# A graph layer on one core: late weights held back, p rows four tiles ahead of q rows, logits split on ScalarE, three double chunks in the tail

## The reference

```python
h = relu(layernorm(x))                                   # x: 256 x 1024
feat = concat([h[src], h[dst]], axis=1)                  # 8448 edges
e_hh = relu(feat[:128] @ W_hh + b_hh)                    # 2048 x 1024 each
e_oo = relu(feat[128:768] @ W_oo + b_oo)
e_ho = relu(feat[768:] @ W_ho + b_ho)
logit = concat([e_hh, e_oo, e_ho]) @ W_a + b_a
alpha = softmax of logit over the edges with one dst
z = segment_sum(alpha * h[src], dst)
h_new = relu(concat([h, z])[:64] @ W_hn + b_hn)
o_new = relu(concat([h, z])[64:] @ W_on + b_on)
x = x + concat([h_new, o_new])
h2 = relu(layernorm(x))
W = zeros(1024, 1024).at[src, dst].add(edge_weight)      # ids are below 256
out = x + h2 @ W.T + bias
```

## Time and profile before

| | us |
|---|---|
| median of 3 runs | 349.29 |
| lowest, highest | 348.75, 351.31 |
| the profiled execution's own time | 351.62 |
| its span, first to last instruction | 349.1 |

### The profile page before, as it was taken

How to read it: one execution, slowest core, us unless ns; L and a number is a source line. 1 busy time by engine, 2 the same in 40 slices (tenths; PEclk the granted TensorE clock), 3 DMA queues, 4 the chain that set the end, 5 groups by cost and what they waited for, 6 DMA issues and landing times.

```text
span 349.1 us, 4052 instructions
## 1 busy us (share of the span) xinstructions
PE 312.1 (89%) x1335; PEld 196.7 (56%) x1335; DVE 262.4 (75%) x475; ACT 161.5 (46%) x343; POOL 161.7 (46%) x148
## 2 busy tenths in 40 slices
PE   0899999998999999999999999999899677479993
PEld 0687688653566665666666665566345535343331
DVE  4737448558927999998899989888975799693315
ACT  3773441642353555485445755535253545424101
POOL 3200077066423787777777777888863300000000
PEclk9999999999999999999999999999999896569997
DMA  7997789999999999999999999999999999970003
GB/s 271 347 353 247 257 324 412 395 279 416 409 408 410 410 408 410 408 410 415 410 409 410 409 414 411 409 408 410 410 409 407 408 410 410 407 318 3 0 0 121
DMA packets 34089, 122.05 MB, mean 350 GB/s; under 512 B 3978, under 2 KB 4362, under 8 KB 34068
## 3 DMA queue, kind: packets, MB, share of 16 engines
q0 software_dynamic: 19008, 69.21, 50.1%
q1 hardware_dynamic: 13668, 47.33, 35.5%
q10 hardware_dynamic: 1392, 5.24, 3.7%
HBM read 115.49 MB, written 6.29 MB: 349 GB/s over the span
## 4 chain that ended last, share of the span: by engine, by line
PE 48%; DMA 23%; POOL 15%; issue 6%; DVE 4%; ACT 2%; POOLq 0%; ACTq 0%; DVEq 0%; SPq 0%
DMA Gp<-p_ho,ids 16%; PE psG L740 12%; PE psG L878 12%; POOL Gq L308 8%; POOL Gp L296 7%; DMA W<-weights 5%; PE psG L846 5%; PE psG L946 4%; PE psW L790 4%; PE psA L790 3%; PE psB L790 2%; PE psG L891 1%; PE psG L896 1%; PE psG L933 1%; DMA xs<-x 1%
## 5 line engine op out<-in xcount | busy, mean ns | idle before, releaser
L308 POOL DMA_INDIRECT Gq<-q_ho,ids x60 | 75.8, 1263 | 54.5 <-DVE Gp L570 28.3
L570 DVE TENSOR_TENSOR Gp<-Gp,Gq 128x1024 f32<-128x1024 f32 x65 | 79.3, 1220 | 21.5 <-DMA Gp<-p_ho,ids 12.7
L296 POOL DMA_INDIRECT Gp<-p_ho,ids x60 | 66.3, 1105 | 44.9 <-DMA p_ho<-T 26.9
L878 PE MATMUL psG<-W,hT 128*128 128x512 f32 x192 | 84.6, 592 | 0.0
L574 DVE SCALAR_TENSOR_TENSOR Gp<-Gp,wa 128x1024 f32<-128x1024 f32 x65 | 79.0, 1215 | 0.1
L410 ACT ACTIVATE RL<-ohs,lgh 128x256 fp32r<-128x256 f32 x66 | 32.9, 499 | 63.9 <-DVE lgl L617 50.7
L878 PEld LDWEIGHTS psG<-W,hT 128*128 128x128 f32 x192 | 35.4, 190 | 40.1 <-issue 40.1
L398 ACT ACTIVATE RW<-ohs,ewh 128x256 fp32r<-128x256 f32 x66 | 33.1, 502 | 45.2 <-DVE ohs L561 29.1
L790 PE MATMUL psA<-RL,ohd 128*128 128x256 f32 x240 | 37.2, 307 | 12.8 <-ACT RL L410 12.6
L790 PE MATMUL psW<-RW,ohd 128*128 128x256 f32 x264 | 46.0, 298 | 0.1
L790 PEld LDWEIGHTS psA<-RL,ohd 128*128 128x128 f32 x240 | 33.3, 206 | 16.2 <-ACT RL L410 14.4
(11 more groups left out here) (147 smaller groups left out, 334.8 us busy)
## 6 DMA issues: line engine op xcount, KB each, us to landing
W<-weights SPq DMA_DIRECT2D x72, 512.0 KB
Gp<-weights SPq DMA_DIRECT2D x8, 512.0 KB, 15.0
xs<-x SPq DMA_DIRECT2D x2, 512.0 KB, 3.7
h_rows<-h ACTq DMA_DIRECT2D x1, 1024.0 KB, 4.7
p_ho<-T ACTq DMA_DIRECT2D x2, 512.0 KB, 4.5
q_ho<-T ACTq DMA_DIRECT2D x2, 512.0 KB, 6.4
p_oo<-T ACTq DMA_DIRECT2D x1, 1024.0 KB
q_oo<-T ACTq DMA_DIRECT2D x1, 1024.0 KB
```

What stands on the lines that cost most here:

```text
L296: nc.gpsimd.indirect_dma_start(out=Gp[:, i % NP, :], out_offset=None, in_=p_oo if t <= OO_TILES else p_ho, in_offset=bass.IndirectOffsetOn ...
L308: nc.gpsimd.indirect_dma_start(out=Gq[:, i % NQ, :], out_offset=None, in_=q_oo if t <= OO_TILES else q_ho, in_offset=bass.IndirectOffsetOn ...
L570: nc.vector.tensor_tensor(Gp[:, i % NP, :], Gp[:, i % NP, :], Gq[:, i % NQ, :], ALU.add).then_inc(s_sum, 1)
L878: last = nc.tensor.matmul(psG[:, 2 * t + half, :], hT[:, k, t * P:(t + 1) * P], W[:, s, half * HALF:(half + 1) * HALF], start=u != 1 and k ...
```

## The change

- `PACE` places 29 jobs instead of 30: one double chunk ahead of each of lots 16, 17 and 18, none ahead of lots 19 and 20, one ahead of each of 21 and 22, and three in the tail.
- SP waits for 56 adds (`LATE_TILES`) ahead of the loads of double chunk 3 (`LATE_TOP`), and for 61 adds (`HN_TILES`) ahead of `hn_w`. SP's order of loads is the same.
- POOL issues twelve p gathers, eight q gathers, and then `q_rows(i)` and `p_rows(i + 4)` in turn.
- `lot_split` leaves DVE. ScalarE copies the lot's logits to a rounded high part, uses the unrounded ones as the scale of the first product (its output is rounded), and makes each low part as an activation of its own. DVE's wait for the products of two lots before now stands ahead of the lot's adds.
- b_a is added to the `off` tables (one more DVE operation in `few_counts`, an activation in place of a multiply in `guard_counts`) instead of to the logits.

```diff
--- before.py
+++ after.py
@@ -51,7 +51,7 @@
 PLAIN = 3 * KC
 JOBS = 4 * KC
 CHUNKS = SPLIT + HH + PLAIN + 2 * KC
-PACE = [2, 2, 2, 2] + [2, 2, 1, 2, 1] + [2, 2, 2, 2] + [2, 1, 1, 1, 1]
+PACE = [2, 2, 2, 2] + [2, 2, 1, 2, 1] + [2, 2, 2, 2] + [1, 1, 1, 0, 0, 1, 1]
 JOBS_IN = [0] * (HH_LOT + 1) + PACE + [0] * (NLOTS - HH_LOT - 1 - len(PACE))
 
 FREED = len(GATHERED) - NP
@@ -66,6 +66,8 @@
 
 
 FREED_Q = len(GATHERED) - NQ
+
+LATE_TOP, LATE_TILES, HN_TILES = 3, 56, 61
 assert FREED_Q % NQ + 3 <= NQ
 assert ROW_SLOT + NT <= NP
 
...
@@ -233,9 +235,12 @@
                     sp.wait_ge(s_lo, q - WSLOTS + 1)
                 else:
                     sp.wait_ge(s_wused, uses_before(q))
+                if q == SPLIT + HH + PLAIN + 2 * LATE_TOP:
+                    sp.wait_ge(s_sum, LATE_TILES)
                 load(q)
                 if q == 2 * WSLOTS:
                     sp.dma_start(wa[:, :], w_a.broadcast_to((P, D))).then_inc(s_wa, 16)
+            sp.wait_ge(s_sum, HN_TILES)
             for k in range(KC):
                 sp.wait_ge(s_used, FREED + k + 1)
                 sp.dma_start(hn_w[k], weights[(CHUNKS + k) * P:(CHUNKS + k + 1) * P, :]).then_inc(s_hn, 16)
@@ -311,11 +316,12 @@
 
             for i in range(NP):
                 p_rows(i)
-            for i in range(NP):
+            for i in range(NQ):
                 q_rows(i)
-            for i in range(NP, len(GATHERED)):
+            for i in range(NQ, len(GATHERED)):
                 q_rows(i)
-                p_rows(i)
+                if i - NQ + NP < len(GATHERED):
+                    p_rows(i - NQ + NP)
 
         @block.scalar
         def _(act):
@@ -399,18 +405,31 @@
                                                     ACT.Copy, scale=val[:, t:t + 1].bitcast(f32))
                     last.then_inc(s_wprod, 1)
 
+            def logit_product(g, i, half, val):
+                n = LTH[LOTS[g][i]]
+                if half == 0 and n >= LRING:
+                    act.wait_ge(s_placed, n - LRING + 1)
+                return nc.scalar.activation(RL[:, n % LRING, half, :], ohs[:, (ENTRY[g] + i) % RING, :].bitcast(f32),
+                                            ACT.Copy, scale=val[:, g % 2, i:i + 1])
+
             def logit_products(g):
 
-                act.wait_ge(s_split, g + 1)
-                for i, t in enumerate(LOTS[g]):
-                    n = LTH[t]
-                    if n >= LRING:
-                        act.wait_ge(s_placed, n - LRING + 1)
-                    for half, val in enumerate((lgh, lgl)):
-                        last = nc.scalar.activation(RL[:, n % LRING, half, :],
-                                                    ohs[:, (ENTRY[g] + i) % RING, :].bitcast(f32), ACT.Copy,
-                                                    scale=val[:, g % 2, i:i + 1].bitcast(f32))
-                    last.then_inc(s_lprod, 1)
+                size, first = len(LOTS[g]), LTH[LOTS[g][0]]
+                if LOTS[g][0]:
+                    act.wait_ge(s_used, PLACE[LOTS[g][-1]] + 1)
+                else:
+                    act.wait_ge(s_hh, 1)
+                nc.scalar.copy(lgh[:, g % 2, 0:size], lg[:, g % 2, 0:size]).then_inc(s_lgh, 1)
+                logit_product(g, 0, 0, lg)
+                act.wait_ge(s_lgh, g + 1)
+                for i in range(size):
+                    nc.scalar.activation(lgl[:, g % 2, i:i + 1], lgh[:, g % 2, i:i + 1].bitcast(f32), ACT.Identity,
+                                         bias=lg[:, g % 2, i:i + 1], scale=-1.0).then_inc(s_lgl, 1)
+                for i in range(size):
+                    if i:
+                        logit_product(g, i, 0, lg)
+                    act.wait_ge(s_lgl, first + i + 1)
+                    logit_product(g, i, 1, lgl).then_inc(s_lprod, 1)
 
             def guard_counts():
 
@@ -419,7 +438,7 @@
                 nc.scalar.activation(inv[:, :, :], psC, ACT.Relu, bias=minus[:, 0:1]).then_inc(s_cm, 1)
                 nc.scalar.activation(off[:, :, :], psC, ACT.Relu, bias=unit[:, 0:1], scale=-1.0).then_inc(s_cm, 1)
                 act.wait_ge(s_cm, 2)
-                nc.scalar.mul(off[:, :, :], off[:, :, :], NEG).then_inc(s_cm, 1)
+                nc.scalar.activation(off[:, :, :], off[:, :, :], ACT.Identity, bias=bar[:, 0:1], scale=NEG).then_inc(s_cm, 1)
 
             def lot_weights(g):
                 if LOTS[g][0] > OO_TILES:
@@ -591,6 +610,8 @@
 
             def lot_logits(g):
 
+                if g >= 2:
+                    dve.wait_ge(s_lprod, LTH[LOTS[g - 2][-1]] + 1)
                 for k, t in enumerate(LOTS[g]):
                     if t and k:
                         total(PLACE[t])
@@ -604,26 +625,13 @@
                     else:
                         hh_logit(col)
 
-            def lot_split(g):
-
-                size = len(LOTS[g])
-                if LOTS[g][0]:
-                    dve.wait_ge(s_used, PLACE[LOTS[g][-1]] + 1)
-                else:
-                    dve.wait_ge(s_hh, 1)
-                if g >= 2:
-                    dve.wait_ge(s_lprod, LTH[LOTS[g - 2][-1]] + 1)
-                chain(nc.vector.tensor_scalar(lgh[:, g % 2, 0:size], lg[:, g % 2, 0:size], bar[:, 0:1], None, ALU.add))
-                nc.vector.scalar_tensor_tensor(out=lgl[:, g % 2, 0:size], in0=lg[:, g % 2, 0:size], scalar=bar[:, 0:1],
-                                               in1=lgh[:, g % 2, 0:size].bitcast(f32), op0=ALU.add, op1=ALU.subtract
-                                               ).then_inc(s_split, 1)
-
             def few_counts():
 
                 dve.wait_ge(s_few, 2)
                 chain(nc.vector.tensor_scalar(inv_few[:, :, :, :], few[:, :, :, :], 1.0, None, ALU.max))
                 chain(nc.vector.reciprocal(inv_few[:, :, :, :], inv_few[:, :, :, :]))
                 chain(nc.vector.tensor_scalar(off_few[:, :, :, :], few[:, :, :, :], 0.5, NEG, ALU.is_lt, ALU.mult))
+                chain(nc.vector.tensor_scalar(off_few[:, :, :, :], off_few[:, :, :, :], bar[:, 0:1], None, ALU.add))
 
             def few_max():
 
@@ -649,7 +657,6 @@
             for g in range(NLOTS):
                 lot_logits(g)
                 lot_start(g + 1)
-                lot_split(g)
                 if g - LAST_OO == 1:
                     few_max()
                 elif g - LAST_OO == 2:
```

More of the change, by code:

```diff
@@ L151, in gnn_block @@
         lgh = sb("lgh", [P, 2, LOT], f32r)
-        lgl = sb("lgl", [P, 2, LOT], f32r)
+        lgl = sb("lgl", [P, 2, LOT], f32)
         brow, ew = shared(("brow", [LOW0 + 32, D], f32), ("ew", [P, ET], f32))
@@ L193, in gnn_block @@
         s_ewh, s_bh, s_bl = sem("weights_high"), sem("biases_high"), sem("biases_low")
-        s_hh, s_split = sem("hh_logit"), sem("logits_split")
+        s_hh, s_lgh, s_lgl = sem("hh_logit"), sem("logits_high"), sem("logits_low")
         s_ohs, s_ohd = sem("src_onehot"), sem("dst_onehot")
```

## The result

| | before | after |
|---|---|---|
| median, us | 350.22 (4 runs, 348.75 to 351.31) | 356.50 (4 runs, 355.03 to 358.50) |
| span of the profiled execution | 349.1 | 353.3 |
| its own time | 351.62 | 355.07 |

The ratio is 1.0186, with a 95% interval of 1.0107 to 1.0265: 6.3 us slower. The median of before moved from 349.29 to 350.22 with a fourth run.

What follows compares the result with a forecast made beforehand. No engine is full over the whole span, so it followed the first AT matmul's start, set by late-arriving bytes and the work left after them. Span 349.1 + 5.1 + 1.5 = 355.7; 6.6 us on the median: 356, range 348 to 361.

Steps and rivals of the forecast that it cites:

- Same bytes, a hole instead: DMA: no byte is added, but its row shows a hole between about 290 and 307 us.
- The hold and the p lead: Gathers behind 240 us, p four tiles ahead, weights later: 50th add at about 250.3 us, last add 47.0 us later.
- The split off DVE: DVE saves 0.4 us per lot: last add starts at 297.3, last logit ends at 299.7, 8.5 us earlier.
- The split on ScalarE, priced at nothing: ScalarE: 24 copies and 66 small activations, at most 26 us on an engine busy 161.5 of 349; taken as nothing.
- P: PE: end of the last placement, forecast at 303 us, 8 us earlier than before.
- The tail: Last placement to first AT matmul: 21.7 us (3.8 + 0.4 + 2.1 + 15.4), before 8.6; AT matmul 5.1 us later.
- The clock: PE idles before the AT matmuls, so its granted clock is low and the first ones longer: 1.5 us, ends 0 and 3.
- The sum: Whole kernel: span 349.1 + 5.1 + 1.5 = 355.7; the shift of 6.6 us put on the median gives 356.
- The rival in which the two effects cancel: Last placement at 294 to 300 us by a smaller cost of the p lead: 346 to 352.5 us; chance 0.25.

Runs made afterwards that it cites:

- scalar_split_only: The kernel before with only the split on ScalarE and b_a in the `off` tables: 353.89 us, ratio 1.0080.
- third_chunk_only: The kernel before with only `PACE` changed, so that three double chunks stand in the tail; no hold: 363.33 us, ratio 1.0319.
- no_hold: The kernel after without the two waits `LATE_TILES` and `HN_TILES`: 359.90 us, ratio 1.0227.
- hold_only: The kernel before with the two waits `LATE_TILES` and `HN_TILES` and the new `PACE`; old gather order, split on DVE: 356.28 us, ratio 1.0123.
- two_in_tail: The kernel after with `PACE` putting chunk 5 ahead of lot 22, so two chunks stand in the tail: 354.82 us, ratio 1.0075.
- hn_before_pair7: The kernel after with SP's loads reordered: `hn_w` from the 59th add, before and after pair 5, then `rows_h`, pair 6, bias row, `x1`, pair 7: 350.72 us, 0.9995.
- pair7_before_x1: hn_before_pair7 with pair 7's load ahead of the bias row and `x1`: 348.0 us, ratio 0.9900.
- pair7_before_x1_two_in_tail: pair7_before_x1 with the `PACE` of two_in_tail (chunk 5 ahead of lot 22): 349.0 us, ratio 0.9929.
- two_in_tail_pair7_early: pair7_before_x1_old_gathers with two_in_tail's `PACE`, pair 6 ahead of `rows_h`, and pair 7 ahead of all wanted only after the AT matmul: 343.18 us, ratio 0.9761.
- p_lead_only: The kernel before with only the new gather order (eight q gathers first, then q of tile i and p of tile i + 4): 350.83 us, ratio 1.0004.
- pair7_before_x1_old_gathers: pair7_before_x1 with before's gather order (q and p of the same tile in turn): 348.0 us, ratio 0.9912.

## Why the prediction was right

The forecast was 356 us; the median is 356.5, and the mechanism is the one it named. Step by step, with times of after's profile. Its clock runs 3.7 us early at the first double chunk (237.09 instead of 240.80), so I give the times from there where that matters.

- **Same bytes, a hole instead.** Right: 122.05 MB in both pages. The forecast hole was 290 to 307 us. Between 290 and 305 us DMA moved 2.07 MB, 138 GB/s on the mean; it thinned out from the 33rd slice on, at about 282.
- **The hold and the p lead.** The 50th add was forecast at 250.3, 9.5 us behind the first double chunk; it started at 245.86, 8.8 behind it. Good to 0.7 us. From there to the last add, forecast 47.0 us, it took 49.5 (245.86 to 295.37). 1.66 us of that is one more wait for q rows, ahead of the 52nd add at 253.00.
- **The split off DVE.** The last add ran without a wait, as the 8.5 us of gain needed.
- **The split on ScalarE, priced at nothing.** The 66 small activations took 279 ns each (294 taken) and the 24 copies 192 ns each. No wait of DVE for them shows among after's waits. The number of table loads stayed at three, with identity now in use. By the Trainium skill's page ScalarE: Activation LUTs, section Table sets: the hidden batching unit, identity is in every set, and the trace agrees, with three loads in both kernels. Put on the kernel before by itself, the split cost 0.8% (scalar_split_only); there the last lots are placed in two pieces and the next chunk starts slowly. In after they go in one, and chunk 5 behind them starts at once with 1.88 us for its first four matmuls.
- **P.** Forecast 303, 62.2 us behind the first double chunk; measured 300.07, 63.0 behind it.
- **The tail.** Forecast 21.7 us from P to the AT matmul, measured 22.7. From the end of chunk 5 at about 303.7 to `rows_h` at 322.6 (309.12 + 13.5) were 19.0 us, against 17.9: the eight `hn_w` issues alone took 4.41 us, and the first slices after the hole are not yet full (240, then 407 GB/s). The rate itself was right: 411 GB/s between 310 and 320 us. The Trainium skill's page DMA: Bandwidth & Descriptors, section Where 436 GB/s comes from, gives about 358 GB/s for such transfers; the full stretches here, at some 410 GB/s, do not bear it out. By that figure these bytes would take 17.6 us, an estimate, against 15.4 at the rate measured.
- **The clock.** Forecast 1.5 us; the first AT matmuls took 3.40 us instead of 1.94, and from there to the end were 30.5 us instead of 29.5. So the term was 1.5 for the AT matmuls alone and 1.0 for the whole end here. In third_chunk_only, no_hold, hold_only and two_in_tail, where PE also idled 9 to 11 us for `rows_h`, the end is longer by 2.1 to 3.4: the first AT matmuls take 3.69 us and the eight behind them 4.36 to 4.86 instead of 3.70.
- **The sum.** 6.6 us forecast; 6.3 between the medians. Within the profiles, from the first double chunk on, 6.9 us to the AT matmul (85.7 instead of 78.8) and 1.0 behind it make 7.9: 0.8 more than forecast up to P, 1.0 more in the tail, 0.5 less for the clock. This execution began its double chunks 3.7 us earlier, so that its span grew by 4.2 only. The mechanism is what was forecast; that the medians agree with the forecast to 0.3 us is partly luck, with runs of one kernel up to 3.5 us apart.

The rival in which the two effects cancel needed a placement at 298 us, or 296.5 with the clock's loss. In after it came at 300.1 on an execution that was 3.7 us early; counted from the first double chunk it is 303.8 on before's scale, some 7 us too late. hn_before_pair7 gets the cancelling in another way: the hole is filled, and its AT matmul starts when before's does.

## What to carry to other kernels

A queue that issues loads in order makes every load wait for the slot of the one ahead. When work is moved behind a point, look for the loads whose slots it frees, and then for all that stands behind those on the queue, wanted or not. On a DMA that is full, moving bytes later wins only if it stays full: order the queue by when each load is wanted, and let no load that waits for a slot stand ahead of loads that could go. An earlier end of one stage is worth nothing until the next thing that the following stage needs is there too.

## What was not expected of the hardware

**SP's queue stood for 13 to 14 us in four profiles.** In two_in_tail, no_hold, pair7_before_x1 and pair7_before_x1_two_in_tail, four of the fourteen, SP's queue waited between 85 and 115 us, in one or two pieces, for something that the profile cannot name. The waits of SP there in two_in_tail (total, times, longest):

```profile
SPq L223 <- PE psG L853: 14.3, 4, 5.0
SPq L223 <- remote: 13.9, 2, 11.4
```

The chain of waits calls it "another core or an unknown queue", from 89.71 us for 11.36 us. The name alone proves little: it also stands on later waits of up to 13.7 us in kernels without the delay, such as two_in_tail_pair7_early. But in the other ten profiles no wait of SP carries it between 80 and 125 us. Meanwhile, in two_in_tail, the queues' even share of the earlier trace rows broke: from 95 to 105 us the gathers had 97% of the DMA engines, and PE and ScalarE also stopped for 1.7 and 1.9 us within their own streams. In the four, the hh product ended at 112 to 114 us instead of 103 to 107, the double chunks began at 246.6 to 252.1 us instead of 237.1 to 242.2, and one or two slices at about 115 to 130 us are below 370 GB/s. What was late was not shown. All four have the p lead, as have four others without the delay; none of the six without the p lead shows it. That may be chance, and no cause is claimed. It may be part of why runs of one kernel lie up to 7.7 us apart (pair7_before_x1_two_in_tail); but those of hold_only, without the p lead, lie 6.6 apart too.

**How fast the first tail chunk starts varies, and how the placements are cut does not tell it.** These are the last placements of six kernels and the four matmuls behind them, from the PE timelines, where no double chunk stands directly ahead:

| kernel | last placements | four matmuls behind, us |
|---|---|---|
| before | twelve, after 5.62 us idle | 2.05 |
| p_lead_only | twelve, after 2.15 idle | 3.03 |
| third_chunk_only | twelve, after 2.15 idle | 3.30 |
| scalar_split_only | eight, 3.06 idle, four | 3.62 |
| pair7_before_x1_old_gathers | eight, 3.59 idle, four | 3.25 |
| two_in_tail_pair7_early | eight, 3.58 idle, four | 2.78 |

Looking at the first and the fourth row alone, one would say that twelve in one piece bring the clock back sooner. The other rows do not agree: one piece gave 3.03 and 3.30, two pieces gave 2.78. What decides it is not shown. Where a double chunk runs directly ahead of the last placements, as in after, the four matmuls took 1.88 us.
